# Row maxima of the scores by four row tiles of 32 rows, two units ahead, in an fp32 cross-attention kernel

## The chip, the cores and the metric

One core of a Trainium2 chip runs the kernel. The time is device microseconds of one execution, as the median of several runs; a profiled execution of the same program gives the trace. TensorE (PE) multiplies, with a record for each weight load (PEld) and each matmul; VectorE (DVE), ScalarE (ACT) and GpSimd (POOL) do the elementwise work, and SyncE (SP) issues the DMAs. Each engine works its own list of instructions in order, and semaphores are all that ties one list to another.

## The reference

Cross-attention with two branches of keys, added, then an output projection with bias and residual:

```python
text, ip = ctx[:, :77, :], ctx[:, 77:, :]          # x (2, 2048, 640), ctx (2, 154, 1024), all f32
q = split_heads(x @ Wq.T, 20)                       # 20 heads of 32
k, v = split_heads(text @ Wk.T, 20), split_heads(text @ Wv.T, 20)
k_ip, v_ip = split_heads(ip @ Wk_ip.T, 20), split_heads(ip @ Wv_ip.T, 20)
attend = lambda q, k, v: softmax(q @ k.T / sqrt(32)) @ v
out = merge_heads(attend(q, k, v)) + merge_heads(attend(q, k_ip, v_ip))
return out @ Wo.T + bo + x
```

## The kernel before

Channels lie on the partitions. A tile is 256 rows of x of one batch, and there are 16. A group is 128 channels, which are four heads of 32, and there are five. A unit is one group of one tile, so there are 80 units, `u`, written out ten at a time (two tiles) in a loop; `u.g` is its group. The softmax subtracts the row maximum of each head, branch and row. The maxima are taken from approximate scores (`q_hi`, the rounded q, against the keys), and enter the exact scores as two more rows of the contraction.

The sequence of each engine is written out by hand in its `emit(u)`, one call a unit, and a step for another unit stands at `u.plus(n)`. In emission u of the kernel before TensorE does, in order: the first two maxima products of u+1 (L735), the exact scores of heads 0 and 1 (L752), 8 of 15 steps of the q product of u+2 (L711), the third maxima product, scores of head 2, the fourth maxima product, more of q, scores of head 3, more of q, the transpose of the maxima of u+1 (L741), the rest of q, the 15 steps of an output chunk of unit u-10 (L711 again, into x_ps), the row sums of u (L769), its product with v (L780), and last the spreading of the inverse sums for unit u-5 (L789).

For a maxima product the kernel keeps `k_diag`, the keys of four heads on the diagonal of a 128 x 308 block with zeros elsewhere. One matmul of 128 x 308 gives the four heads of one branch for 128 rows; the two branches and the two halves of the tile make four matmuls a unit, which take turns in two PSUM banks, `a_ps`. VectorE reduces each (L571).

Once a tile, at `u.g == 0`, the row sums of the tile before are turned into inverses: ScalarE's `keep_sums` copies them (L422, behind the first two exponentials L405 and `keep_pv` L410), VectorE's `invert_sums` takes the reciprocal (L585) and splits it (L588, L590), which gives `inv_done`. The spread for group 0 of that tile waits for `inv_done`:

```python
def spread_inverse(u):
    if u.g == 0:
        wait(pe, inv_done, u.tile(INV_STEPS, INV_STEPS))
    wait(pe, scaled_done, u.number())
    wait(pe, y_done, u.number(1, 1 + SPREAD_LAG - OUT_LAG))
    spread_matmuls(u, x_ps)
```

VectorE's `normalise` (L598) then multiplies the spread inverses with the product with v. Every value for a product is kept as a rounded high part and a low part (fp32r), so that each product of q and of the output is 15 steps. Before the loop stand the key and value products of the context; in the first five units ScalarE and VectorE also split Wo (L464, L554).

Of the kernel before, what the change touches and what calls it, by code (L numbers as in the profile page):

```python
# [50 lines left out]
BLK = GROUP * KEYS  # L51
# [4 lines left out]
MAXES = SUB * BRANCHES  # L56
A_ITEMS = MAXES + 1
# [43 lines left out]
def build(nc, x_d, ctx_d, wq_d, wk_d, wv_d, wo_d, bo_d, out_d):  # L101
    with ExitStack() as stack:
# [20 lines left out]
        k_diag = sbuf("k_diag", [P, BRANCHES, GROUPS, BATCHES, GROUP, KEYS], F32R)  # L123
# [50 lines left out]
        zeroed = sem("zeroed")  # L174
# [20 lines left out]
        a_ready, a_drained = sem("a_ready"), sem("a_drained")  # L195
# [18 lines left out]
        K_ITEMS = BRANCHES * GROUPS  # L214

# [30 lines left out]
        def _(sp):  # L246
# [23 lines left out]
            def maxima(u):  # L270


                wait(sp, a_drained, u.number(A_ITEMS, A_ITEMS))
                sp.dma_start(q_stack[SHIFT_ROW:STACK, u.slot].bitcast(F32),
                             max_rows[:, u.slot, :].bitcast(F32)).then_inc(max_in[u.slot], DMA)
# [43 lines left out]
        def _(pool):  # L319
# [10 lines left out]
            nc.gpsimd.memset(k_diag[:, 1].bitcast(F32), 0.0).then_inc(zeroed, 1)  # L330
# [43 lines left out]
            add_branches(LAST.plus(-1))  # L374
# [9 lines left out]
        def _(act):  # L384
            def q_high(u):

                wait(act, q_acc, u.number(1, 1))
                wait(act, a_ready, u.number(A_ITEMS, -A_ITEMS))
# [77 lines left out]
            def keys_high(item):  # L466
# [5 lines left out]
                for j in range(GROUP):  # L472
                    rows = slice(j * D, (j + 1) * D)
                    done = nc.scalar.activation(
                        k_diag[rows, br, g, :, j, :],
                        k_banks[br][g % 2][rows, group_cols(g)].rearrange("p (b n) -> p b n", b=BATCHES),
                        ACT.Copy, scale=SCALE)
                done.then_inc(k_hi_done, 1)

            def keys_top(item):  # L480
# [3 lines left out]
                for j in range(GROUP):  # L484
                    nc.scalar.activation(k_stack[0:D, br, g * GROUP + j],  # L485
                                         k_diag[j * D:(j + 1) * D, br, g, :, j, :].bitcast(F32),
# [22 lines left out]
            act.wait_ge(zeroed, 2)  # L509
# [33 lines left out]
        def _(dve):  # L543
            nc.vector.memset(k_diag[:, 0].bitcast(F32), 0.0).then_inc(zeroed, 1)
# [21 lines left out]
            def max_piece(u, k):  # L566

                sub, br = divmod(k, BRANCHES)
                wait(dve, a_ready, u.number(A_ITEMS, k + 1))
                bank = a_ps[(u.c * A_ITEMS + k) % 2]  # L570
                nc.vector.tensor_reduce(row_max[:, u.slot, br, :, sub],  # L571
# [431 lines left out]
```

## Time and profile before

| | |
|---|---|
| time, median of 3 | 685.42 us (683.55 to 728.46) |
| the profiled execution's own time | 683.04 us |
| its span in the trace | 681.2 us |
| its mean granted TensorE clock | 0.989 of full |
| PE busy | 657.5 us, 97% of the span |
| DVE busy | 435.7 us, 64% |
| ACT busy | 493.3 us, 72% |
| POOL busy | 225.0 us, 33% |

The time is a little more than the span, which runs from the first to the last record. The row to look at is PE: matmul records overlap each other, so 97% says that TensorE hardly ever waits, and not that it is at its peak. The clock of the trace has two levels, 1.2 and 2.4 GHz, shown as 0.50 and 1.00.

### The profile page before, as it was taken

The page shows a single profiled execution, that of the slowest core. Times are in us where ns is not written, and L with a number is a line of the kernel's source. Part 1 is how long each engine was busy: PE and PEld are TensorE (multiplying, and loading weights), DVE is VectorE, ACT ScalarE, POOL GpSimd, SP SyncE. Part 2 cuts the span into 40 slices and gives each one's busy share as a digit, 9 for nine tenths or more (in the row PEclk, how much of TensorE's full clock was granted, in tenths as well). Part 3 has the DMA queues.
Part 4 walks back from the last instruction along what each step waited for, and adds up shares of the span by engine and source line. Part 5 has one row for each costly group of instructions (what it writes and reads, how often), then busy time and mean ns, then how long its engine had stood idle before and what let it go on. Part 6 is the DMA issues. An engine that isn't in the chain of part 4 may idle for free.

```text
span 681.2 us, 18904 instructions
## 1 busy us (share of the span) xinstructions
PE 657.5 (97%) x6514; PEld 564.5 (83%) x6514; DVE 435.7 (64%) x956; ACT 493.3 (72%) x1078; POOL 225.0 (33%) x261
## 2 busy tenths in 40 slices
PE   9959798999999999999999999999999999999997
PEld 9959576788888888888888888888888888888877
DVE  6786677675757566675756576665657566756633
ACT  3983787877868777877777787778777777876730
POOL 4020102243432434343434324343434243342333
PEclk9989898999999999999999999999999999999999
DMA  8950111223131221313131312213131323212212
GB/s 318 410 234 9 25 56 34 80 57 96 49 103 51 82 63 55 93 48 97 51 93 49 99 55 86 55 55 93 48 101 51 90 55 93 56 50 64 56 42 69
DMA packets 34691, 57.46 MB, mean 84 GB/s; under 512 B 4832, under 2 KB 27232, under 8 KB 34400
## 3 DMA queue, kind: packets, MB, share of 16 engines
q1 hardware_dynamic: 34656, 56.99, 27.3%
q8 instruction: 22, 0.36, 0.2%
q14 instruction: 13, 0.11, 0.0%
HBM read 35.34 MB, written 10.49 MB: 67 GB/s over the span
## 4 chain that ended last, share of the span: by engine, by line
PE 85%; DVE 6%; ACT 6%; issue 2%; POOL 0%; DVEq 0%; ACTq 0%
PE q_ps L711 19%; PE x_ps L711 19%; PE sum_ps L769 11%; PE b_ps L752 10%; PE pv_ps L780 10%; PE a_ps L735 7%; PE x_ps L789 5%; PE a_ps L741 1%; ACT probs L405 1%; DVE k_stack L631 1%; DVE k_stack L641 1%; ACT k_stack L485 1%; ACT q_stack L397 1%; DVE wo_lo L554 1%; DVE k_stack L545 1%
## 5 line engine op out<-in xcount | busy, mean ns | idle before, releaser
L405 ACT ACTIVATE probs<-b_ps 77x512 f32<-77x512 f32 x320 | 181.1, 591 | 121.0 <-PE b_ps L752 119.3
L562 DVE TENSOR_TENSOR q_stack<-q_ps,q_hi 32x256 fp32r<-32x256 f32 x320 | 134.3, 420 | 36.0 <-ACT q_hi L390 32.3
L571 DVE TENSOR_REDUCE row_max<-a_ps 128x4 f32<-128x308 f32 x320 | 137.6, 471 | 24.0 <-PE a_ps L735 21.3
L397 ACT ACTIVATE q_stack<-q_hi 32x256 fp32r<-32x256 f32 x320 | 133.0, 416 | 10.0
L598 DVE TENSOR_TENSOR scaled<-x_ps,pv_sb 128x512 f32<-128x512 f32 x75 | 51.9, 692 | 105.4 <-PE x_ps L789 105.0
L752 PE MATMUL b_ps<-q_stack,k_stack 98*77 98x256 f32 x640 | 115.1, 281 | 0.5 <-ACT probs L405 0.5
L347 POOL TENSOR_TENSOR scaled<-scaled 128x256 f32<-128x256 f32 x80 | 59.2, 740 | 139.1 <-DVE scaled L598 139.0
L352 POOL TENSOR_TENSOR attn_lo<-scaled,attn_hi 128x256 fp32r<-128x256 f32 x80 | 59.1, 739 | 113.2 <-ACT attn_hi L434 113.2
L358 POOL TENSOR_TENSOR res<-y,res 128x256 f32<-128x256 f32 x70 | 51.1, 731 | 136.8 <-ACT y L428 136.8
L735 PE MATMUL a_ps<-k_diag,q_hi 128*128 128x308 f32 x320 | 87.3, 313 | 7.0 <-DVE row_max L571 6.8
L752 PEld LDWEIGHTS b_ps<-q_stack,k_stack 98*77 98x77 f32 x640 | 85.7, 146 | 1.5 <-ACT probs L405 1.0
L711 PE MATMUL q_ps<-x_lo,wq_hi 128*128 128x256 f32 x400 | 86.7, 283 | 0.0
L780 PE MATMUL pv_ps<-probs,v 128*32 128x256 f32 x1280 | 84.3, 381 | 0.0
L769 PE MATMUL sum_ps<-probs,sum_one 128*32 128x256 f32 x1152 | 79.7, 390 | 1.2 <-ACT probs L405 1.2
L711 PE MATMUL q_ps<-x_hi,wq_hi 128*128 128x256 f32 x400 | 74.4, 283 | 6.6 <-POOL x_lo L341 6.3
L711 PE MATMUL q_ps<-x_hi,wq_lo 128*128 128x256 f32 x400 | 80.2, 298 | 0.0
L341 POOL TENSOR_TENSOR x_lo<-x_raw,x_hi 128x1280 fp32r<-128x1280 f32 x16 | 49.1, 3066 | 60.0 <-ACT x_hi L416 60.0
L711 PE MATMUL x_ps<-attn_hi,wo_hi 128*128 128x256 f32 x365 | 66.7, 280 | 0.8 <-DVE scaled L598 0.8
L711 PEld LDWEIGHTS q_ps<-x_lo,wq_hi 128*128 128x128 f32 x400 | 67.1, 192 | 0.0
L711 PE MATMUL x_ps<-attn_lo,wo_hi 128*128 128x256 f32 x365 | 66.6, 280 | 0.2 <-POOL attn_lo L352 0.2
L711 PE MATMUL x_ps<-attn_hi,wo_lo 128*128 128x256 f32 x365 | 66.5, 280 | 0.0
L780 PEld LDWEIGHTS pv_ps<-probs,v 128*32 128x32 f32 x1280 | 42.0, 111 | 28.4 <-issue 1.4
(111 smaller groups left out, 962.3 us busy)
## 6 DMA issues: line engine op xcount, KB each, us to landing
x_raw<-x_in SPq DMA_DIRECT2D x16, 640.0 KB, 4.2
q_stack<-q_stack SPq DMA_DIRECT2D x80, 128.0 KB, 2.3
res<-x_in SPq DMA_DIRECT2D x75, 128.0 KB, 2.0
y_out<-res SPq DMA_DIRECT2D x75, 128.0 KB, 1.7
stage<-wk_in SPq DMA_DIRECT2D x6, 640.0 KB, 7.9
stage<-wv_in SPq DMA_DIRECT2D x6, 640.0 KB, 10.7
wq_raw<-wq_in SPq DMA_DIRECT2D x1, 1600.0 KB, 10.2
wo_raw<-wo_in SPq DMA_DIRECT2D x1, 1600.0 KB, 14.6
```

Source lines behind the costliest of these rows:

```text
L347: nc.gpsimd.tensor_tensor(scaled[:, s, 0:N], scaled[:, s, 0:N], scaled[:, s, N:2 * N], ALU.add).then_inc(attn_done, 1)
L352: nc.gpsimd.tensor_tensor(attn_lo[:, u.batch, u.g, :], scaled[:, u.slot, 0:N], attn_hi[:, u.batch, u.g, :].bitcast(F32), ALU.subtract).the ...
L397: done = nc.scalar.activation(q_stack[0:D, u.slot, j, :], q_hi[j * D:(j + 1) * D, u.slot, :].bitcast(F32), ACT.Copy)
L405: nc.scalar.activation(probs[0:KEYS, j, :], b_ps[j % 2][0:KEYS, :], ACT.Exp).then_inc(b_drained, 1)
L562: done = nc.vector.tensor_tensor(q_stack[D:2 * D, u.slot, j, :], q_ps[rows, 0:N], q_hi[rows, u.slot, :].bitcast(F32), ALU.subtract)
L571: nc.vector.tensor_reduce(row_max[:, u.slot, br, :, sub], bank[:, 0:BLK].rearrange("p (j n) -> p j n", j=GROUP), AXIS.X, ALU.max).then_inc ...
L598: nc.vector.tensor_tensor(scaled[:, u.slot, :], bank[:], pv_sb[:, u.g, :], ALU.mult).then_inc(scaled_done, 1)
L711: return nc.tensor.matmul(out, (lo if kind == 1 else hi)(k), (moving_lo if kind == 2 else moving_hi)(k), start=(n == 0), stop=(n == STEPS_ ...
L735: nc.tensor.matmul(a_ps[(u.c * A_ITEMS + k) % 2][:, 0:BLK], q_hi[:, u.slot, sub * P:(sub + 1) * P], k_diag[:, br, u.g, u.batch].rearrange( ...
L752: done = nc.tensor.matmul(b_ps[j % 2][0:KEYS, br * N:(br + 1) * N], k_stack[0:STACK, br, u.g * GROUP + j, u.batch, :], q_stack[0:STACK, u. ...
L769: nc.tensor.matmul(sum_ps[j * D:(j + 1) * D, 0:N], sum_first[:] if first else sum_one[:, D - 1 - c:2 * D - 1 - c], probs[:, j, br * N:(br ...
L780: done = nc.tensor.matmul(pv_ps[j * D:(j + 1) * D, br * N:(br + 1) * N], v[:, br, u.batch, h * D:(h + 1) * D], probs[:, j, br * N:(br + 1) ...
```

## The change

Zero blocks go: `k_heads` holds the keys of a group as they come, 128 partitions with the four heads at 32 partitions each, both branches side by side. A maxima product is now one head, 32 rows deep, 128 rows of q wide, with 154 columns moving (77 keys of two branches). Eight such matmuls make a unit; four in turn lie in different row groups of the array and write to four PSUM banks (`b_ps` and `a_ps`). They come in one block, for unit u+2 and not u+1, between the output chunk and the row sums. VectorE's four reductions follow the low part of q. The spread goes from the end of the emission to between the q product and the output chunk, into the second `a_ps` bank and not `x_ps`; normalise follows in the same emission and not in the next, at group 0 behind `invert_sums`. Before the loop, two memsets of `k_diag` and three of four ScalarE copies of each key item go, and the maxima of unit 1 are made there.

```diff
-MAXES = SUB * BRANCHES
-A_ITEMS = MAXES + 1
+MAX_ITEMS = GROUP + 1
-        k_diag = sbuf("k_diag", [P, BRANCHES, GROUPS, BATCHES, GROUP, KEYS], F32R)
+        k_heads = sbuf("k_heads", [P, GROUPS, BATCHES, BRANCHES, KEYS], F32R)
+        max_banks = [*b_ps, *a_ps]
...
 gpsimd emit(u)
-                ahead, norm, chunk = u.tile_plus(1), u.plus(-1 - SPREAD_LAG), u.plus(-OUT_LAG)
+                ahead, norm, chunk = u.tile_plus(1), u.plus(-SPREAD_LAG), u.plus(-OUT_LAG)
+                if norm.plus(-1).exists():
+                    attn_low(norm.plus(-1))
                 if norm.exists():
                     add_branches(norm)
-                    attn_low(norm)
...
 scalar keys_high(item)
-                for j in range(GROUP):
-                    rows = slice(j * D, (j + 1) * D)
-                    done = nc.scalar.activation(
-                        k_diag[rows, br, g, :, j, :],
-                        k_banks[br][g % 2][rows, group_cols(g)].rearrange("p (b n) -> p b n", b=BATCHES),
-                        ACT.Copy, scale=SCALE)
-                done.then_inc(k_hi_done, 1)
+                nc.scalar.activation(k_heads[:, g, :, br, :],
+                                     k_banks[br][g % 2][:, group_cols(g)].rearrange("p (b n) -> p b n", b=BATCHES),
+                                     ACT.Copy, scale=SCALE).then_inc(k_hi_done, 1)
...
 vector
+            def max_piece(u, j, bank):
+                if not (u.fixed and u.number() == 0):
+                    wait(dve, max_ready, u.number(1, 1))
+                nc.vector.tensor_reduce(row_max[:, u.slot, :, j, :].rearrange("p r s -> p s r"),
+                                        bank[:, 0:SUB * BLK].rearrange("p (s r n) -> p s r n", s=SUB, r=BRANCHES),
+                                        AXIS.X, ALU.max).then_inc(max_read, 1)
...
             def emit(u):
-                norm, nxt = u.plus(-1 - SPREAD_LAG), u.plus(1)
-                if norm.exists():
-                    normalise(norm)
-                if nxt.exists():
-                    for k in range(MAXES):
-                        max_piece(nxt, k)
-                    max_turned(nxt)
+                norm, nxt = u.plus(-SPREAD_LAG), u.plus(1)
+                if nxt.exists():
+                    max_turned(nxt)
+                if norm.exists() and u.g != 0:
+                    normalise(norm)
                 if u.g == 0 and u.tile_plus(-1).exists():
                     invert_sums(u.tile_plus(-1))
+                if norm.exists() and u.g == 0:
+                    normalise(norm)
                 if u.plus(2).exists():
                     q_low(u.plus(2))
+                    for j in range(GROUP):
+                        max_piece(u.plus(2), j, max_banks[j])
...
 tensor
+            def max_matmuls(u, heads, banks):
+                for sub in range(SUB):
+                    for j, bank in zip(heads, banks):
+                        rows = slice(j * D, (j + 1) * D)
+                        done = nc.tensor.matmul(bank[:, sub * BLK:(sub + 1) * BLK],
+                                                q_hi[rows, u.slot, sub * P:(sub + 1) * P],
+                                                k_heads[rows, u.g, u.batch].rearrange("p r n -> p (r n)"),
+                                                start=True, stop=True, skip_group_check=True)
+                return done
+
+            def max_scores(u):
+                wait(pe, q_hi_done, u.number(1, 1))
+                wait(pe, max_read, u.number(MAX_ITEMS))
+                wait(pe, scaled_done, u.number(1, -1 - SPREAD_LAG))
+                wait(pe, b_drained, u.number(GROUP, -GROUP))
+                max_matmuls(u, range(GROUP), max_banks).then_inc(max_ready, 1)
...
 scores(u, j)
+                if j < 2 and u.plus(1).exists():
+                    wait(pe, max_read, u.number(MAX_ITEMS, MAX_ITEMS + j + 1))
...
 spread_inverse(u)
                 wait(pe, scaled_done, u.number())
-                wait(pe, y_done, u.number(1, 1 + SPREAD_LAG - OUT_LAG))
-                spread_matmuls(u, x_ps)
+                if u.plus(SPREAD_LAG + 1).exists():
+                    wait(pe, max_read, u.number(MAX_ITEMS, (SPREAD_LAG + 1) * MAX_ITEMS + GROUP))
+                spread_matmuls(u, a_ps[1])
...
 emit(u)
-                find_max(0)
-                find_max(1)
                 scores(u, 0)
+                project_q(u.plus(2), 0, 3)
                 scores(u, 1)
-                project_q(u.plus(2), 0, 8)
-                find_max(2)
+                project_q(u.plus(2), 3, 7)
+                if nxt.exists():
+                    turn_maxima(nxt)
                 scores(u, 2)
-                find_max(3)
-                project_q(u.plus(2), 8, 10)
+                project_q(u.plus(2), 7, 11)
                 scores(u, 3)
-                project_q(u.plus(2), 10, 13)
-                find_max(MAXES)
-                project_q(u.plus(2), 13)
+                project_q(u.plus(2), 11)
+                if norm.exists():
+                    spread_inverse(norm)
                 if chunk.exists():
                     project_out(chunk)
+                if u.plus(2).exists():
+                    max_scores(u.plus(2))
                 row_sums(u)
                 weigh_values(u)
-                if norm.exists():
-                    spread_inverse(norm)
...
 before the loop
+            pe.wait_ge(max_read, MAX_ITEMS)
+            wait(pe, q_hi_done, 2)
+            max_matmuls(first.plus(1), range(GROUP), max_banks).then_inc(max_ready, 2)
```

In the changed kernel BLK is 154 (`BRANCHES * KEYS`); it was 308.

## Rows read from the trace of the kernel before

**Rows 1.** Part 1 of the page: engine, busy us, share, instructions.
```profile
PE   657.5 (97%) x6514; PEld 564.5 (83%) x6514; DVE 435.7 (64%) x956; ACT 493.3 (72%) x1078; POOL 225.0 (33%) x261
```

**Rows 2.** Busy time by stage: window, us, then engines' busy us, PEclk.
```profile
302.00:377.00 75.00, 75.00 (x774) 64.21 (x773) 47.74 (x107) 57.29 (x126) 27.80 (x32) 1.00 0.25 71
```

**Rows 3.** Waits of TensorE over the span: total us, times, longest.
```profile
PE a_ps L735 <- DVE row_max L571: 6.8, 5, 3.9
```

**Rows 4.** Timeline of TensorE over one unit: start us, us, engine, line, records.
```profile
404.40 0.51 PE L789 MATMUL x_ps<-inv_parts,spread 128*128 128x256 f32 x2
...
409.88 0.28 PE L711 MATMUL x_ps<-attn_lo,wo_hi 128*128 128x256 f32 x1
410.10 1.07 PE L769 MATMUL sum_ps<-probs,sum_one 128*32 128x256 f32 x16
410.98 1.05 PE L780 MATMUL pv_ps<-probs,v 128*32 128x256 f32 x16
411.96 0.51 PE L789 MATMUL x_ps<-inv_parts,spread 128*128 128x256 f32 x2
412.31 0.44 PE L735 MATMUL a_ps<-k_diag,q_hi 128*128 128x308 f32 x2
412.59 0.64 PE L752 MATMUL b_ps<-q_stack,k_stack 98*77 98x256 f32 x4
413.06 0.64 PE L711 MATMUL q_ps<-x_hi,wq_hi 128*128 128x256 f32 x4
```

**Rows 5.** Weight loads by form: records, busy us, mean ns of one.
```profile
L711 PEld LDWEIGHTS q_ps<-x_hi,wq_hi 128*128 128x128 f32 x400 | 59.2, 190 | 7.3 <-issue 6.5 <-DVE q_stack L562 0.8
...
L741 PEld LDWEIGHTS a_ps<-ident,row_max 128*16 128x16 f32 x80 | 7.0, 88 | 0.6 <-DVE row_max L571 0.6
```

**Rows 6.** Timeline of weight loads, windows 395.07 to 395.09 and 395.11 to 395.13.
```profile
395.08 0.11 PEld L769 LDWEIGHTS sum_ps<-probs,sum_one 128*32 128x32 f32 x2
395.08 0.16 PEld L769 LDWEIGHTS sum_ps<-probs,sum_one 128*32 128x32 f32 x8
```

**Rows 7.** Timeline of TensorE before the loop, products with 154 columns moving.
```profile
57.69 1.47 PE L913 MATMUL b_ps<-ctx,stage 128*128 128x154 f32 x10
58.99 0.27 PE L741 MATMUL a_ps<-ident,row_max 128*16 128x128 f32 x1
```

**Rows 8.** Timeline of a unit of group 0, from its first scores on.
```profile
397.58 0.63 PE L752 MATMUL b_ps<-q_stack,k_stack 98*77 98x256 f32 x4
398.01 1.08 ACT L405 ACTIVATE probs<-b_ps 77x512 f32<-77x512 f32 x2 [0.62 <-PE b_ps L752]
...
399.46 0.39 ACT L422 ACTIVATE inv<-sum_ps 128x256 f32<-128x256 f32 x1
...
400.33 0.27 PE L741 MATMUL a_ps<-ident,row_max 128*16 128x128 f32 x1
...
400.94 1.73 DVE L585 RECIPROCAL inv<-inv 128x256 f32<-128x256 f32 x1
...
403.03 0.49 DVE L590 SCALAR_TENSOR_TENSOR inv_parts<-inv_hi,low_rows,inv 128x256 fp32r<-128x256 f32 x1
```

**Rows 9.** Timeline of TensorE in the first units: waits in brackets.
```profile
78.13 0.41 PE L735 MATMUL a_ps<-k_diag,q_hi 128*128 128x308 f32 x1 [3.86 <-DVE row_max L571]
...
105.43 0.41 PE L735 MATMUL a_ps<-k_diag,q_hi 128*128 128x308 f32 x1 [1.66 <-DVE row_max L571]
```

**Rows 10.** Busy time and clock by microsecond, columns as in Rows 2.
```profile
106.00:107.00 1.00, 1.00 (x9) 0.97 (x9) 0.74 (x2) 0.86 (x2) 0.00 (x0) 0.86 0.07 16
107.00:108.00 1.00, 1.00 (x9) 0.74 (x10) 0.52 (x2) 0.42 (x2) 0.00 (x0) 0.50 0.00 0
...
110.00:111.00 1.00, 1.00 (x17) 0.47 (x10) 0.95 (x3) 0.08 (x1) 0.00 (x0) 0.94 0.00 0
```

**Rows 11.** Timeline before and at the start of the loop.
```profile
47.04 1.19 PE L711 MATMUL q_ps<-x_hi,wq_hi 128*128 128x256 f32 x4 [6.30 <-POOL x_lo L341]
...
74.59 2.98 DVE L554 TENSOR_TENSOR wo_lo<-wo_raw,wo_hi 128x640 fp32r<-128x640 f32 x1 [1.99 <-ACT wo_hi L464]
```

More of the change, by code:

```diff
@@ L50 @@
 UNITS = TILES * GROUPS
-BLK = GROUP * KEYS
+BLK = BRANCHES * KEYS
 SHIFT_ROW = 3 * D
@@ L270, in maxima @@
             def maxima(u):
-                wait(sp, a_drained, u.number(A_ITEMS, A_ITEMS))
+                wait(sp, max_read, u.number(MAX_ITEMS, MAX_ITEMS))
                 sp.dma_start(q_stack[SHIFT_ROW:STACK, u.slot].bitcast(F32),
@@ L387, in q_high @@
                 wait(act, q_acc, u.number(1, 1))
-                wait(act, a_ready, u.number(A_ITEMS, -A_ITEMS))
+                wait(act, max_ready, u.number(1, -1))
                 wait(act, q_low_done, u.number(1, -1))
@@ L591, in invert_sums, with normalise @@
                                                in1=inv[:], op0=ALU.mult, op1=ALU.add).then_inc(inv_done, 1)
-            def normalise(u, bank=x_ps):
+            def normalise(u, bank=a_ps[1]):
                 wait(dve, inv_spread, u.number(1, 1))
@@ L671, in _ @@
             nc.vector.memset(probs[64:P], 0.0).then_inc(probs_zeroed, 1)
-            for k in range(MAXES):
-                max_piece(Unit(0, 0), k)
+            for j in range(GROUP):
+                dve.wait_ge(first_max_ready, j // 2 + 1)
+                max_piece(Unit(0, 0), j, a_ps[j % 2])
             dve.wait_ge(v_zeroed, 1)
@@ L682, in _ @@
                 place_v(item)
+            for j in range(GROUP):
+                max_piece(Unit(0, 1), j, max_banks[j])
             dve.wait_ge(bo_loaded, DMA)
@@ L686, in _ @@
             stages(emit)
-            normalise(LAST.plus(-1))
             invert_sums(LAST)
@@ L727, in project_q @@
                     done.then_inc(q_acc, 1)
-            def max_scores(u, k):
-                sub, br = divmod(k, BRANCHES)
-                if k == 0:
-                    wait(pe, q_hi_done, u.number(1, 1))
-                wait(pe, a_drained, u.number(A_ITEMS, k - 1))
-                nc.tensor.matmul(a_ps[(u.c * A_ITEMS + k) % 2][:, 0:BLK], q_hi[:, u.slot, sub * P:(sub + 1) * P],
-                                 k_diag[:, br, u.g, u.batch].rearrange("p j n -> p (j n)"),
-                                 start=True, stop=True).then_inc(a_ready, 1)
+            def max_matmuls(u, heads, banks):
[13 more added lines that the diff above has]
+                max_matmuls(u, range(GROUP), max_banks).then_inc(max_ready, 1)
             def turn_maxima(u):
-                wait(pe, a_drained, u.number(A_ITEMS, MAXES))
-                nc.tensor.transpose(a_ps[(u.c * A_ITEMS + MAXES) % 2][0:BRANCHES * SUB * GROUP, 0:P],
-                                    row_max[:, u.slot].rearrange("p r j s -> p (r j s)"), ident[:]).then_inc(a_ready, 1)
+                wait(pe, max_read, u.number(MAX_ITEMS, GROUP))
+                nc.tensor.transpose(a_ps[0][0:BRANCHES * SUB * GROUP, 0:P],
+                                    row_max[:, u.slot].rearrange("p r j s -> p (r j s)"), ident[:]
+                                    ).then_inc(max_turned_over, 1)
             def scores(u, j):
@@ L948, in _ @@
             project_ip_values(1, 4)
-            max_scores(first, 0)
-            max_scores(first, 1)
+            wait(pe, q_hi_done, 1)
+            max_matmuls(first, (0, 1), a_ps).then_inc(first_max_ready, 1)
             project_ip_values(4, 5)
-            max_scores(first, 2)
-            max_scores(first, 3)
+            wait(pe, max_read, 2)
+            max_matmuls(first, (2, 3), a_ps).then_inc(first_max_ready, 1)
             project_ip_values(5, 6)
```

33 lines of the change are left out of this document (10 added, 23 removed).

## The prediction

> **What bounds the kernel now.** I read the page's busy times first: TensorE is busy 657.5 of 681.2 us and no other engine over 72% [rows 1]. The window of a middle stretch says it harder: 75.00 of 75.00 us busy at clock 1.00 [rows 2]. The view of waits then shows what TensorE waited for: its largest item is 6.8 us in five waits, the maxima products for VectorE's reductions [rows 3], and the two that the timeline places at 78.13 and 105.43 make 5.5 of them, in the first units [rows 9]. So in the loop the time is the sum of TensorE's own steps, and every wait that the change puts into TensorE's list is paid in full.
>
> The timeline gives the price of each step as distance from start to start, since records overlap. A unit lasts 411.96 - 404.40 = 7.56 us; four score matmuls take 413.06 - 412.59 = 0.47, or 0.117 each (256 columns, fp32r); two maxima matmuls of 308 columns take 0.28, or 0.14 each; the row sums 0.88 for 16 records, the product with v 0.98, the two spread matmuls 0.35; the last output step to the first sum 0.22 where 0.12 would be its own share [all rows 4]. The 0.10 beyond it, the 0.98 against 0.88, and the 0.35 against 2 x 0.117 are what a change of the array's tiling costs: about 0.10 before the first load, and for a 128-column load another 0.12 that no matmul hides.
>
> **The change part by part.**
>
> *Maxima on TensorE.* Gone: 4 x 0.14 = 0.56 us a unit [rows 4]. New: eight matmuls of 154 columns in two rounds of four. No row tile stands in the trace, so I bound it. The nearest rows are the column tiles of the row sums: eight weight loads start within 0.05 us (0.16 less the 0.11 of one), some 7 ns apart [rows 6], and 16 records of 256 columns take 0.88 us, a quarter of what they would one after another [rows 4]. If row tiles do the same, a round costs what one matmul does. A load costs by its width: (190 - 88) ns for 112 more columns [rows 5], so about 0.12 us for 128. One pass over 154 columns is 154/256 of 0.117, 0.07 us. The block: first load 0.12, second load 0.12 (the first round lies under it), second round 0.07, sum 0.31. It has another tiling than the output chunk and than the row sums, so there are two changes where there was one: +0.10. The spread, now between two products of the full array, loses its 0.12 of bare load; instead the scores follow the product with v and bare a 77-column load, +0.07. In all -0.56 + 0.31 + 0.10 - 0.12 + 0.07 = -0.20 a unit. The steps of the old unit add up to 39 x 0.117 (30 product, 8 score and the transpose) + 0.56 + 0.35 + 0.10 + 0.88 + 0.98 = 7.43, so 0.13 of this 7.56 was small waits, mostly of the two-bank ping-pong of maxima and reductions; the unit before took less, so I count 0.05 of them, and they go. That makes -0.25 x 80 = -20 us.
>
> The other end has two places. The same trace runs a product of 154 columns in plain f32 as two records of (58.99 - 57.69)/10 = 0.13 [rows 7], 0.26 a product; all its fp32r products move 256 columns or more. If fp32r at 154 columns is run like f32, the block is 0.12 + 2 x 0.26 = 0.64 and not 0.31, +26 us over 80 units. If the eight 128-column loads go one after another, it is 8 x 0.12 + 0.07 = 1.03, +58 us. Below 0.31 nothing goes much: the gain would be 0.56 + 0.05 at most with a free block, 0.3 more than I take. I take 0.31 since the column tiles are the nearest rows.
>
> The Trainium skill's page "TensorE: Matmul & The Clock Gate", section "What overlaps and what doesn't", speaks against it: a weight load overlaps matmuls in flight only where its row group differs. The second round's loads would then wait for the first round, 0.38 for the block and 5 us more in all. The trace shows the contrary where it can: loads of the same column tile start before its matmul has run [rows 6], so I leave the sum as it is.
>
> *Two units ahead, and four banks.* Reductions are four of about the same size as before. Max_scores waits for the rounded q, for the reads of u+1's maxima and their transpose, for normalise of u-5 (it read that bank), and for the last exponential. By TensorE's list there are a spread and an output chunk, 0.23 + 1.76 = 2 us, between the q product and it, against one ScalarE copy or one normalise of under 0.7; no wait. The next unit's first scores wait for the first reduction; row sums and product with v, 1.9 us, cover it and q_low's four pieces. In the first ten units, without chunks, the cover is thinner. Cost nothing, 1 us at most a unit of those.
>
> *The spread moved forward.* This is the step that decides. In group-0 units the spread needs `inv_done` of the tile before, whose chain starts in the same emission. From the unit's first scores at 397.58: first exponential at +0.43, keep_sums at +1.88, the transpose of the maxima at +2.75, the reciprocal at +3.36 behind the turned maxima, the last step ends at 403.03 + 0.49, +5.94 [rows 8]. The spread was at 404.40, +6.82, so 0.88 us in hand. In the new order: scores of head 1 start at 0.23 + 0.35 = 0.58, so the second exponential at 1.01, keep_pv 1.49, keep_sums 1.97. Reciprocal to end of the split is 2.58 in the trace; VectorE is free after the turned maxima (transpose at 1.28, read till about 1.96), so the reciprocal starts 0.4 behind the copy, at 2.4, and inv_done comes at 4.96, TensorE goes on at 5.05. But it arrives at 8 scores, 15 q steps and a transpose, 24 x 0.117 = 2.8. Wait: 2.25 us, behind which the whole output chunk, the maxima, sums and product with v are queued, and ScalarE and VectorE behind those. TensorE has no slack to give it back. Tiles with such a spread inside the loop: 15 (units 5, 10, ... 75). +34 us. In the other four groups the spread waits for nothing late.
>
> *The clock.* Behind the wait of 1.66 us at 105.43 the granted clock goes to 0.50 (1.2 GHz) from about 106.7 to 110.1 [rows 9, 10]: 3.4 us at half speed, 1.7 us lost. The new waits are longer, 2.25, and come once in five units. I count the fall behind 12 of 15, since one row is thin evidence for each: 12 x 1.7 = +20 us; bounds 0 and 15, +26.
>
> *Start.* ScalarE's key copies fall from four to one an item and two memsets go, which pulls forward the low part of x that TensorE waited 6.30 us for at 47.04 [rows 11]. But TensorE's wait of 3.86 at 78.13 is for VectorE, busy with the low part of Wo until 77.57, and that waited for ScalarE and its input [rows 9, 11]; what is gained before runs into it. New order leaves it somewhat further in its list by then, and the wait of 1.66 falls in with the first new one. Against it, the first scores of unit 0 now wait for the first reduction of unit 1. I take -4, bounds 0 and -9.
>
> Sum against the profiled execution's 683.0: -20 - 4 + 34 + 20 = +30, 713 us. The median of the runs shown is 685.4, 0.3% above that execution, so it is the same measure.
>
> **Rivals.**
>
> *The clock stays up.* All as above, but waits of 2.25 us don't bring it down: 683 - 20 - 4 + 34 = 693, range 688 to 699, +1% and so not slower by what can be told. For it: a busy block before and behind each wait. Against: the row at 106.7. It decides at how many of the 15 the clock falls; below 4 of them the result is under 699.
>
> *f32 pace at 154 columns.* +26 on the forecast: 739 (719 with the clock up). For it: no fp32r row under 256 columns. Against: the type, not the width, parts the rows there are.
>
> *Loads one after another.* +58: 771 (751 with the clock up). For it: a load's time goes by its width. Against: the column tiles' loads.
>
> *The other side.* TensorE reaches the spread late instead of waiting there. Scores of heads 2 and 3 wait for the first two exponentials, and head 0 for the DMA of the maxima; were TensorE held at one of these in every group-0 unit by 2 us while ScalarE, already past the exponentials, goes on with keep_sums, the chain would be as good as done on arrival. It decides from a rest of the wait under 0.5 us; that leaves 7 of the 34 us, no fall of the clock, and 683 - 20 - 4 + 7 = 666. Against it: the DMA is asked for 1 us earlier in the unit than now, and by the new order the exponentials end (1.0 and 1.6) before the scores that need them (1.4 and 2.1).
>
> **How the numbers follow.** Forecast 713 (701 to 722): 0.45. Clock up: 0.16. f32 pace: 0.15. Loads in turn: 0.13. Wait absent or small: 0.05. Else, spread about: 0.06. Low 688 takes in the clock rival, high 752 the f32 pace and the mild end of the loads rival; left out are the 666 case and most of the loads rival, about 0.18. Some two per cent is what a measurement of this kernel can tell from no change: faster (under 671.7) 0.05, within (to 699.1) 0.21, slower 0.74.
>
> **What would show it.** The spread record (L789's like) of every fifth unit with an idle of about 2.25 us before it, released by the split of the inverse on VectorE, 15 times; ScalarE's keep_sums some 2 us and the reciprocal some 2.4 us behind the unit's first scores. Granted clock 0.50 for 3.4 us behind most of them, mean near 0.96 in the loop. Ordinary units of 7.2 to 7.3 us. The maxima block, from its first load to the first load of the row sums, 0.3 + 0.1; eight records of 154 columns each, starting in fours some 7 ns apart. Records in twos would be f32 pace, starts 0.1 apart would be loads in turn. I am wrong if the chain's end comes before TensorE arrives, or if max_scores or the first scores wait for reductions in ordinary units.

## The result, and the profile after

The changed kernel takes 730.84 us, median of four, against 685.07: ratio 1.0676, interval 1.064 to 1.0712. One of the four executions of the kernel before was a slow one of 728.46 us, and the ratio leaves it out (the other three have a median of 684.72). The changed kernel's profiled execution took 729.86, its span is 728.1 us at a mean granted clock of 0.957, against 681.2 at 0.989.

The view of waits, beside [rows 3], tells most of it (engine, line, who was waited for: total us, times, longest):

```profile
PE a_ps L799 <- DVE inv_parts L584: 27.0, 15, 2.2
PE b_ps L762 <- issue: 14.9, 5, 3.0
PE b_ps L732 <- DVE scaled L592: 4.9, 5, 1.0
PE q_ps L709 <- POOL x_lo L342: 3.7, 1, 3.7
```

The first row is the forecast wait of the spread, 15 times. The second stands in no part of the prediction: TensorE stops before the first scores of a loop pass, five times for about 3 us, and the profile shows no other engine that it waits for ("issue"). From here on it is called the stop at the back edge, which is the jump from the end of a pass to the start of the next. The third is the maxima product of units 5 to 9, which waits for normalise.

All rows of that view add up to 60.1 us; for the kernel before they make 19.4. The clock's loss is (1 - 0.957) x 728.1 = 31.3 us against (1 - 0.989) x 681.2 = 7.5. So of 728.1 - 681.2 = 46.9 us, 40.7 are waits, 23.8 are clock, and the rest, -17.6, is what is left for faster work.

An ordinary unit, beside [rows 4], timeline of TensorE (start us, us):

```profile
402.52 0.40 PE L799 MATMUL a_ps<-inv_parts,spread 128*128 128x256 f32 x2
402.75 0.64 PE L709 MATMUL x_ps<-attn_hi,wo_hi 128*128 128x256 f32 x4
...
404.42 0.28 PE L709 MATMUL x_ps<-attn_lo,wo_hi 128*128 128x256 f32 x1
404.63 0.34 PE L732 MATMUL b_ps<-k_heads,q_hi 32*128 32x154 f32 x2
404.63 0.34 PE L732 MATMUL a_ps<-k_heads,q_hi 32*128 32x154 f32 x2
404.80 0.27 PE L732 MATMUL b_ps<-k_heads,q_hi 32*128 32x154 f32 x2
404.81 0.27 PE L732 MATMUL a_ps<-k_heads,q_hi 32*128 32x154 f32 x2
405.01 1.07 PE L779 MATMUL sum_ps<-probs,sum_one 128*32 128x256 f32 x16
...
409.78 0.40 PE L799 MATMUL a_ps<-inv_parts,spread 128*128 128x256 f32 x2
```

Read the starts: from spread to spread 7.26 us. The unit of [rows 4] took 7.56, but it is the longest of its tile: five units of the kernel before, from the scores at 397.58 to those at 434.94, take 37.36 us, 7.47 each. The two spreads take 0.23 (before 0.35); four maxima matmuls start together at 404.63, the second four at 404.80, and the sums at 405.01. From 404.63 to 405.01, less the 0.10 of the next change of tiling, is 0.28 us for eight matmuls. They are one record each, where plain f32 had two [rows 7], so fp32r with 154 columns is one pass here.

Their loads, beside [rows 6]:

```profile
404.63 0.18 PEld L732 LDWEIGHTS b_ps<-k_heads,q_hi 32*128 32x128 f32 x2
404.63 0.18 PEld L732 LDWEIGHTS a_ps<-k_heads,q_hi 32*128 32x128 f32 x2
404.73 0.19 PEld L732 LDWEIGHTS b_ps<-k_heads,q_hi 32*128 32x128 f32 x2
404.74 0.19 PEld L732 LDWEIGHTS a_ps<-k_heads,q_hi 32*128 32x128 f32 x2
```

Four loads of 128 columns start within 0.01 us, four more 0.10 later, while the first matmuls still run by their records: row tiles load side by side as the column tiles do.

A unit of group 0, beside [rows 8]:

```profile
421.41 0.46 PE L762 MATMUL b_ps<-q_stack,k_stack 98*77 98x256 f32 x2
...
423.47 0.38 ACT L423 ACTIVATE inv<-sum_ps 128x256 f32<-128x256 f32 x1
...
423.88 1.75 DVE L579 RECIPROCAL inv<-inv 128x256 f32<-128x256 f32 x1 [0.43 <-ACT inv L423]
...
424.19 0.28 PE L709 MATMUL q_ps<-x_lo,wq_hi 128*128 128x256 f32 x1
...
426.00 0.48 DVE L584 SCALAR_TENSOR_TENSOR inv_parts<-inv_hi,low_rows,inv 128x256 fp32r<-128x256 f32 x1
426.53 0.70 PE L799 MATMUL a_ps<-inv_parts,spread 128*128 128x256 f32 x2 [2.06 <-DVE inv_parts L584]
```

Against the first scores: keep_sums at +2.06 (forecast 1.97), reciprocal +2.47 (2.4), spread +5.12 (5.05). The wait reads 2.06 since the profile counts it from the end of the last matmul's record; from that matmul's start, 424.19, to the spread's are 2.34 us, less the 0.12 that a step takes 2.22, and the forecast was 2.25.

In the first unit of a pass it looks otherwise:

```profile
299.79 0.46 PE L762 MATMUL b_ps<-q_stack,k_stack 98*77 98x256 f32 x2 [2.97 <-issue]
300.08 0.61 PE L709 MATMUL q_ps<-x_hi,wq_hi 128*128 128x256 f32 x3
...
304.09 0.28 PE L709 MATMUL q_ps<-x_lo,wq_hi 128*128 128x256 f32 x1
305.46 0.50 PE L799 MATMUL a_ps<-inv_parts,spread 128*128 128x256 f32 x2 [1.10 <-DVE inv_parts L584]
```

The inverse is no earlier here (spread at +5.67), but TensorE has come to it later: its last step ends at +4.57 where it ended at +3.06 above, for behind the stop it runs at half clock.

And the clock behind such waits, beside [rows 10] (window, us, engines' busy us, PEclk):

```profile
263.00:265.00 2.00, 2.00 (x10) 1.79 (x9) 1.86 (x5) 0.00 (x0) 0.73 (x1) 0.50 0.29 66
306.00:308.00 2.00, 2.00 (x23) 1.82 (x21) 1.85 (x4) 0.94 (x3) 0.73 (x1) 1.00 0.12 25
427.00:429.00 2.00, 2.00 (x12) 2.00 (x11) 1.58 (x4) 0.17 (x1) 0.73 (x1) 0.50 0.29 66
634.00:636.00 2.00, 2.00 (x27) 1.70 (x29) 1.93 (x5) 0.48 (x1) 0.74 (x1) 1.00 0.33 74
```

In the two microseconds behind the 15 waits it stood at 0.50 nine times and at 1.00 six times; behind all five stops at the back edge it stood at 0.50. One of the nine lies in a stretch that a stop had begun (215.0 to 225.3). Of the ten waits of 2.06 to 2.24 us seven had the half clock behind them.

### The profile page after: what moved, and what is told of

Read it like the earlier page. It is cut to its first block, busy times and chain, and to the rows that moved or that the text cites. A ratio compares the mean times of both kernels' runs of the same rounds, so it can differ in the third digit from the quotient of the medians.

```text
span 728.1 us, 19277 instructions
## 1 busy us (share of the span) xinstructions
PE 662.8 (91%) x6834; PEld 559.5 (77%) x6834; DVE 433.8 (60%) x955; ACT 481.3 (66%) x1048; POOL 221.6 (30%) x260
## 4 chain that ended last, share of the span: by engine, by line
PE 76%; DVE 13%; issue 5%; ACT 3%; DMA 1%; SPq 0%; DVEq 0%; ACTq 0%; POOL 0%
PE x_ps L709 17%; PE q_ps L709 17%; PE b_ps L762 11%; PE sum_ps L779 10%; PE pv_ps L790 9%; PE b_ps L732 4%; DVE inv L579 4%; PE a_ps L799 3%; DVE q_stack L557 2%; DVE k_stack L637 2%; DVE row_max L565 1%; DVE k_stack L627 1%; PE a_ps L918 1%; PE a_ps L748 1%; DVE inv_parts L584 1%
## 5 line engine op out<-in xcount | busy, mean ns | idle before, releaser
L406 ACT ACTIVATE probs<-b_ps 77x512 f32<-77x512 f32 x320 | 189.1, 594 | 149.3 <-PE b_ps L762 148.2
L762 PE MATMUL b_ps<-q_stack,k_stack 98*77 98x256 f32 x640 | 143.4, 307 | 18.8 <-issue 14.9
L592 DVE TENSOR_TENSOR scaled<-a_ps,pv_sb 128x512 f32<-128x512 f32 x75 | 51.9, 692 | 96.2 <-PE a_ps L799 96.2
L573 DVE CAST max_rows<-a_ps 16x128 fp32r<-16x128 f32 x80 | 22.3, 278 | 134.6 <-PE a_ps L748 134.6
L709 PE MATMUL q_ps<-x_hi,wq_hi 128*128 128x256 f32 x400 | 89.0, 289 | 3.7 <-POOL x_lo L342 3.7
L709 PE MATMUL q_ps<-x_hi,wq_lo 128*128 128x256 f32 x400 | 88.8, 289 | 0.0
L565 DVE TENSOR_REDUCE row_max<-b_ps 128x4 f32<-128x308 f32 x158 | 68.4, 475 | 10.2 <-PE a_ps L732 8.0
L709 PE MATMUL x_ps<-attn_lo,wo_hi 128*128 128x256 f32 x365 | 71.0, 294 | 0.3 <-POOL attn_lo L353 0.3
L709 PEld LDWEIGHTS q_ps<-x_hi,wq_hi 128*128 128x128 f32 x400 | 66.8, 196 | 4.0 <-issue 3.9
L565 DVE TENSOR_REDUCE row_max<-a_ps 128x4 f32<-128x308 f32 x162 | 69.3, 471 | 0.6 <-PE a_ps L732 0.5
```

Of the source, the lines that this page charges most:

```text
L406: nc.scalar.activation(probs[0:KEYS, j, :], b_ps[j % 2][0:KEYS, :], ACT.Exp).then_inc(b_drained, 1)
L565: nc.vector.tensor_reduce(row_max[:, u.slot, :, j, :].rearrange("p r s -> p s r"), bank[:, 0:SUB * BLK].rearrange("p (s r n) -> p s r n", ...
L592: nc.vector.tensor_tensor(scaled[:, u.slot, :], bank[:], pv_sb[:, u.g, :], ALU.mult).then_inc(scaled_done, 1)
L709: return nc.tensor.matmul(out, (lo if kind == 1 else hi)(k), (moving_lo if kind == 2 else moving_hi)(k), start=(n == 0), stop=(n == STEPS_ ...
L762: done = nc.tensor.matmul(b_ps[j % 2][0:KEYS, br * N:(br + 1) * N], k_stack[0:STACK, br, u.g * GROUP + j, u.batch, :], q_stack[0:STACK, u. ...
```

## The experiments

Each was measured beside the kernel before on the same chip; that one's medians there were 683.6 to 684.5 us. "Records" are those of TensorE in one pass of the loop, with its weight loads and those instructions for waiting and counting that the trace records. "Packets" are the transfers of instructions over the whole execution, about 16 KB each (22 make 0.36 MB in the kernel before).

**e1: the spread back at the end.** PE emission (normalise, GpSimd and the guarding waits follow as in the kernel before):

```diff
-                if norm.exists():
-                    spread_inverse(norm)
                 if chunk.exists():
                     project_out(chunk)
...
                 weigh_values(u)
+                if norm.exists():
+                    spread_inverse(norm)
```

> The changed kernel with one part undone: the spread of the inverse sums stands again at the end of the emission, into the bank of the output chunk, and normalise follows in the next emission, as before the change; the row tiles, four banks and two units ahead stay. My account of the changed kernel's 730.8 us: 15 waits for the inverse, 27.0 us in its trace; five waits of 0.99 us of the maxima for normalise in units 5 to 9; the clock at half for 61 us against 14 before, which loses 24 us more than before; and five stops of 3 us at the loop's back edge put down to issue. Theory A (the waits and the clock falls behind them are the spread's place): the 15 and the five waits go, most clock falls with them, the stops at the back edge stay, the spread bares its weight load again (+7): 730.8 - 27 - 5 - 19 + 7 = about 687 us. Rival B (the clock falls come from the row tiles, not from the waits): the half-clock stretches stay, about 706 us. Rival C (another wait takes their place, since the inverse was only the first of several late steps): 715 us or more.

Measured 689.23 us, ratio 1.0083 (1.0061 to 1.0105). No wait for the inverse is left; this is:

```profile
PE b_ps L760 <- issue: 15.2, 6, 3.1
PE b_ps L731 <- ACT q_hi L391: 6.5, 9, 1.0
```

The clock is 0.986 over 687.3 us, a loss of 9.6 and not 31.3. Theory A, 2 us above its 687: 42 us of the result belong to the spread's place, and about half of them are clock. The waits of units 5 to 9 stayed in another form (for the rounded q: 6.5 us against 1.9 in the changed kernel), where A had them go. The stops stayed, and four of the five long ones have a half-clock stretch behind them.

**e2: fewer waits in TensorE's loop.** In `max_scores`, `scores` and `spread_inverse`, waits implied by others stand only outside the loop (`u.fixed` is true there), as in

```diff
-                wait(pe, b_drained, u.number(GROUP, -GROUP))
+                if u.fixed:
+                    wait(pe, b_drained, u.number(GROUP, -GROUP))
```

> The changed kernel, with seven waits a unit left out of TensorE's list inside the loop, each met already by an earlier wait of the same list or chain, so nothing else moves. TensorE's loop body has 1620 matmul and load records as before this edit, but by the program some 100 instructions fewer in all, about as many as the kernel before has. The changed kernel stops five times for 3 us at the loop's back edge, and its trace shows instruction transfers all through the loop, 68 packets against 22 of the kernel before, which shows none between 213 and 595 us. Theory A (the body has outgrown what stays resident, and is fetched again in each pass): stops and transfers go, 5 x 3.0 us and the half-clock stretch behind each (5 x 1.7 at most): 707 to 716 us. Rival B (the stops come from the new order, whatever the length): within 2 us of 730.8, transfers unchanged. Rival C: the edit isn't large enough, transfers and stops stay, 726 to 731 us.

726.20 us, ratio 1.0613 (1.0572 to 1.0655). Five stops, 14.8 us, 67 packets: rival C. The edit made 1738 records a pass out of 1780.

**e3: the wait filled with work.**

```diff
+FILL = 19
...
                 if u.g == 0:
+                    wait(pe, y_done, u.number(1, SPREAD_LAG - OUT_LAG))
+                    for _ in range(FILL):
+                        nc.tensor.matmul(x_ps[:, 0:N], wq_hi[:, 0, 0:P], x_hi[:, u.batch, 0, :], start=True, stop=True)
                     wait(pe, inv_done, u.tile(INV_STEPS, INV_STEPS))
```

> The changed kernel with 19 matmuls of no use (256 columns, into the output chunk's bank, before the chunk starts) ahead of each spread of group 0, so that TensorE works where it waited for the inverse; the wait for the inverse follows them. Nothing of the result changes. 19 x 0.117 = 2.2 us, as long as the wait. Theory A (idle time of 2 us brings the clock down, and that costs 1.7 us each): the waits shrink to under 0.3 us, as much time is used as before the edit, but the half-clock stretches behind them go, 11 or so of 15: 730.8 - 15 to -19 = 712 to 716 us. Rival B (the clock goes down whatever TensorE does there): 730 to 733 us with as many half-clock stretches. Rival C: the matmuls delay the inverse chain itself: over 735 us.

733.73 us, ratio 1.0714 (1.0693 to 1.0736), where A said 712 to 716 and B 730 to 733. One of the four executions took 3223.3 us; it has no trace, and what it did is open (the other three: 733.03 to 734.00). The time misses A by 18 us and lies nearest to B, and the trace says otherwise. First its clock behind two filled waits, then its waits:

```profile
432.00:434.00 2.00, 2.00 (x19) 1.97 (x18) 1.27 (x4) 0.73 (x2) 0.50 (x1) 1.00 0.09 23
264.00:266.00 2.00, 2.00 (x40) 1.08 (x40) 1.96 (x6) 0.43 (x1) 0.73 (x1) 1.00 0.04 8
```

```profile
PE b_ps L763 <- issue: 15.4, 5, 3.3
PE q_ps L710 <- issue: 9.2, 5, 2.0
```

No wait for the inverse, and no fall of the clock behind any of the 15; the loss by clock is (1 - 0.973) x 732.2 = 19.8 us and not 31.3. But 78 records more in a pass come with a second stop behind the first, 9.2 us. Fill +33.6 (15 x 2.24), waits -27.0, clock -11.5, second stop +9.2: +4.3, and the spans differ by 4.1 (the fit is closer than its terms, for a wait that reads 2.06 costs 2.2 from start to start). So it is the idle time that brings the clock down. A had priced the clock only: a fill longer than the waits that it replaced, and the second stop, took back what the clock gave.

**e4: the kernel before, with a longer loop.**

```diff
+PAD = 9
...
                 row_sums(u)
+                if not u.fixed:
+                    for _ in range(PAD):
+                        wait(pe, b_drained, u.number(GROUP, 1))
                 weigh_values(u)
```

> The kernel before, with nine more waits a unit in TensorE's list inside the loop, all on a semaphore value that is met already, 90 instructions a pass of ten units, so that the loop body is as long as the changed kernel's. Theory A (length alone makes the loop fetch its instructions anew and stop at the back edge): transfers of instructions all through the loop, five stops of about 3 us, perhaps a half-clock stretch behind each: 685 + 15 to + 24 = 700 to 709 us. Rival B (length is harmless, the stops belong to the new order): 685 to 687 us, no transfers between 213 and 595 us. If the waits themselves take time in TensorE's list, 0.05 us each, up to 27 us more appear as longer units, and the trace tells them apart.

Median 705.37 us of 708.28, 708.80, 702.46 and 688.66, too far apart for a ratio. Only the first was traced: it has four stops, 14.8 us, 58 packets and 1739 records. That the one of 688.66 us ran without stops is likely by its clock (0.990 against 0.972) and not shown. The trace has both cases in itself, though: between 444 and 527 us no instructions are transferred, and the back edge in that stretch, at 452, is the one without a stop. So the stops need nothing of the change, and they come and go with the transfers. The 90 waits more a pass are only 50 records more: a record isn't an instruction, and all counts below are of records.

**e5: e1 with a shorter loop.** Edit as in e2, on e1, for nine waits.

> The kernel of e1 (spread at the end of the emission again), with nine waits a unit less in TensorE's loop, each implied by another wait that stays. e1 measured 689.2 us; of that, five or six stops of 3 us at the loop's back edge (15.2 us in its trace) and three half-clock stretches behind them. Its loop pass had 1769 TensorE records, the kernel before 1689 without a stop, e2 1738 and the lengthened kernel before (e4) 1739 with stops. This one should have about 1715. Theory A (a body of so many records stays resident): no instruction transfers inside the loop, 689 - 15 - 5 = 667 to 671 us, which would be 2% faster than before. Rival B (the limit lies below 1715): stops stay, 685 to 689 us. Rival C (a wait left out did hide something): slower than 690 us.

690.87 us, ratio 1.0107 (1.009 to 1.0124), 1722 records, five stops, 13.3 us. The time is 2 us over B's range and just in that of rival C; by the trace it is B, the stops stay. Of what C supposes the trace shows little: 4.9 us of waits of the first scores for VectorE's reductions, against 3.0 in e1. Leaving waits out gives nothing by itself either.

**e6: the heads in turn.**

```diff
-                for sub in range(SUB):
-                    for j, bank in zip(heads, banks):
+                for j, bank in zip(heads, banks):
+                    for sub in range(SUB):
```

> The kernel of e1, with the eight maxima matmuls of a unit in another order: the two halves of one head one behind the other, then the next head, so that matmuls next to each other lie in the same row group. Same instructions, same number. In e1 the four heads start within 0.02 us. Theory A (four row tiles run side by side only if they follow each other; TensorE starts in order): the second matmul of a head waits for its own load, 0.12 us, and holds the next head back; the block takes about 0.6 us and not 0.28, +0.3 x 80 = 24 us, 710 to 716 us. Rival B (the array sorts it out, loads of other row groups run ahead): 0.3 us, 688 to 691 us.

690.66 us, ratio 1.01 (1.0083 to 1.0117), within 1.5 us of e1: rival B. Its timeline:

```profile
406.06 0.28 PE L708 MATMUL x_ps<-attn_lo,wo_hi 128*128 128x256 f32 x1
406.27 0.34 PE L731 MATMUL b_ps<-k_heads,q_hi 32*128 32x154 f32 x2
406.29 0.34 PE L731 MATMUL a_ps<-k_heads,q_hi 32*128 32x154 f32 x2
406.45 0.28 PE L731 MATMUL b_ps<-k_heads,q_hi 32*128 32x154 f32 x2
406.46 0.28 PE L731 MATMUL a_ps<-k_heads,q_hi 32*128 32x154 f32 x2
406.67 0.64 PE L777 MATMUL sum_ps<-probs,sum_first 128*32 128x256 f32 x8
```

0.40 us from the first to the sums, where the order by halves takes 0.38. Neighbours in the list need not lie in different row groups.

**e7: only group 0 back.** As e1, but `if u.g == 0` at the end and `u.g != 0` in the middle, with the banks to match, and eleven waits left out.

> The changed kernel, with the spread at the end of the emission (into the output chunk's bank, normalise in the next emission) only in units of group 0, where the inverse comes late; in the other four groups it stays between the q product and the output chunk. Eleven or so waits a unit less in TensorE's loop, each implied by another, about 1708 records a pass. Theory A: no wait for the inverse, no stop at the back edge; against e5 four of five spreads keep their load covered, 0.1 us each, 60 of them, 6 us less: 661 to 665 us. Rival B (as for e5: the body is still too long): 680 to 684 us. Rival C (normalise of group 0 now meets that of group 1 in one emission and pushes VectorE or GpSimd late): over 690 us.

688.68 us, ratio 1.0067 (1.005 to 1.0085), 1711 records, five stops, 14.8 us. By the stops it is rival B, but 5 us over its 680 to 684: the rest of the edit saves 2 us against e5, where I had reckoned with 6.

**e8, e9, e10: only the place of the loop.** After eight kernels with the stop, of 1711 to 1858 records, against one of 1689 without, it was either the length or the place of the body in the list. Small matmuls go before the loop, 44 in e8 (on e2), 48 in e9 (on e7), 35 in e10 (on the kernel before):

```diff
             project_ip_values(0, 1)
+            for _ in range(44):
+                nc.tensor.matmul(q_ps[0:16, 0:16], ident[:, 0:16], ident[:, 0:16], start=True, stop=True)
             pe.wait_ge(wq_lo_done, 1)
```

> The kernel of e2 with nothing changed in the loop: 44 matmuls of no use (16 columns, f32, four records each) stand before the loop, where TensorE waits for the low part of x anyway, and shift its list by 176 records. Counted in blocks of 256 records (an instruction transfer is 16 KB, 64 bytes each), the loop of the kernel before began at 8.02 and ended at 14.61, seven blocks, 8 to 14, and was not fetched again. Those of the changed kernel (8.41 to 15.36), e1 (8.45 to 15.36), e2 (8.41 to 15.20), e5 (8.42 to 15.14) and e7 (8.40 to 15.09) touch eight blocks, and all stop at the back edge; e4 began at 7.98. This one goes from 9.10 to 15.89, seven blocks, with e2's body of 1738. Theory A (seven blocks stay, eight don't): no transfers inside the loop, no stops, 726.2 - 14.8 - about 7 of clock = 703 to 707 us. Rival B (it is the number of records in the body, limit between 1693 and 1711): stops stay, 724 to 729 us.

> The kernel of e7, its loop untouched, with 48 such matmuls before the loop: its start goes from 8.40 to 9.15 blocks and its end to 15.84, seven blocks instead of eight. Theory A (blocks touched): 688.7 - 14.8 for the stops - up to 8.5 for half-clock stretches (20.4 us of them against 3.4 where nothing stops) = 664 to 669 us, 2 to 3% faster than the kernel before. Rival B (length of the body): 687 to 690 us.

> The kernel before, its loop untouched, with 35 such matmuls before the loop, where TensorE waits 6.3 us anyway: start from 8.02 to 8.56 blocks, end from 14.61 to 15.16, eight blocks instead of seven. Theory A: transfers of instructions all through the loop, stops of 3 to 4 us at the back edge, half-clock stretches behind some: 684 + 15 to + 24 = 699 to 708 us. Rival B (length of the body): 683 to 686 us, no transfers between 213 and 595 us.

e8: 725.87 us, ratio 1.0613 (1.0583 to 1.0642). e9: 691.50 us, 1.0109 (1.0092 to 1.0126). Both with stops (14.5 and 14.4 us); e8 is in rival B's range, e9 1.5 us over it. e10: 711.31 us, 1.0399 (1.0382 to 1.0417), 3 us over theory A's 699 to 708, and this one rules rival B out, for its loop is that of the kernel before, instruction for instruction. Its waits, and its transfers of instructions on the page (queue: packets, MB, share):

```profile
PE a_ps L735 <- issue: 16.9, 9, 3.0
PE a_ps L735 <- DVE row_max L571: 6.9, 5, 3.8
```

```profile
q8 instruction: 67, 1.10, 0.6%
```

The same line of the kernel before has 22 packets, none of them between 202 and 585 us. The added matmuls take 1.9 us inside a wait for x that was there before. By the spans it is 29.9 us longer than the kernel before: 16.9 are stops, 11.0 clock by the means. So the place decides. What was wrong in e8 and e9 may then be only the zero of my count, and e11 tests that.

**e11 and e12: the place worked out from the failures.**

> The kernel of e7 once more, loop untouched, now with 30 small matmuls before the loop (e9 had 48). e10 showed that a shift alone of the kernel before, with the same body, brings the stops; e8 and e9 showed that the block borders don't lie where whole numbers of my count lie. If seven blocks stay and eight don't, the runs bound the place of the border in the count: before (8.02 to 14.61) without stops puts it at a fraction between .62 and 1.02; e9 (9.15 to 15.84) with stops takes away all from .83 up, e4 (7.98 to 14.79) all from .79. So a border lies at a fraction of .62 to .79. This kernel goes from 8.87 to 15.55, which is seven blocks for every border in that stretch. Theory A (blocks touched): no transfers inside the loop, no stops, 688.7 - 14.8 - 5 to 8.5 = 664 to 669 us, 2 to 3% faster than before. Rival B (a shift matters in another way, or 1711 records are too many wherever they lie): 687 to 692 us.

669.43 us, ratio 0.9781 (0.9765 to 0.9798): 2.2% faster than the kernel before, and 19 us less than e7 with the same loop. Its packets and its largest waits:

```profile
q8 instruction: 23, 0.38, 0.3%
```

```profile
PE b_ps L772 <- DVE row_max L567: 5.9, 14, 1.9
PE b_ps L735 <- ACT q_hi L393: 4.2, 7, 1.0
```

No stop at the back edge; from 215 to 595 us the clock is 1.00. With e7 and e9 this is one loop at three places: 688.68, 691.50 and 669.43 us.

> The kernel of e2 (order of the changed kernel, waits for the inverse and all; seven redundant waits a unit left out), with 28 small matmuls before the loop: from 8.85 to 15.64 in my count, seven blocks for a border at a fraction of .63 to .79. e11 fell from 688.7 to 669.4 us by the same kind of shift, e8 (44 of the matmuls, wrong place) not at all. Theory A: no transfers in the loop, no stops at the back edge, 726.2 - 19 = 705 to 709 us; what then stays above the kernel before, 21 to 25 us, is the price of the moved spread less the gain of the row tiles. The half-clock stretches behind the waits for the inverse stay. Rival B (with the inverse waits in, the stop at the back edge only hides another wait of the same length): 715 us or more.

714.78 us, ratio 1.0424 (1.0357 to 1.0491), executions from 709.03 to 718.82. Between the two theories by its median: the profiled execution has two stops, 8.3 us, in the first passes, then none (41 packets, none between 371 and 616 us). Its loop is e2's, 1738 records, and by the count it ends at 15.64, 0.09 blocks beyond e11, so it left little room below eight blocks; e4, just as tight, varied in the same way. That tight fits settle late is what these two suggest and is not shown further. Once the stops are gone the wait for the inverse is 2.08 us in the first unit of a pass too, and a pass takes 78.6 us (spreads at 385.33, 463.95, 542.56) where the kernel before takes 74.7. So the moved spread costs about 4 us a pass, clock included, after the gain of the row tiles; for 80 units that is an estimate of 31.

## Why the prediction was right, and what it left out

- *The spread's place* decided, as said. Forecast 15 waits of 2.25, 34 us; there were 15, ten of 2.06 to 2.24 and five, in the first units of the passes, of 0.7 to 1.7: 27.0 us. These five are shorter since TensorE reached the spread late, at half clock behind the stop, and not since the inverse was early. e1 shows that without the 15, and with the clock back, 42 us go.
- *The clock.* Forecast: 12 falls of the 15, +20 us. Found: behind the 15 waits eight half-clock stretches of their own, 15.4 us lost (the ninth wait fell into a stop's stretch), and behind the stops another 11.9. That the whole came to +23.8 and so near to 20 is luck: one part was counted too high and the other not at all. e3 shows that idle time does it: with work in the wait it never fell there.
- *The row tiles.* Forecast 0.31 us for the block, found 0.28; a unit 0.25 us less, found 0.22 (7.47 to 7.25), which makes 17.6 us over 80 units, as much as the rest above. Both rivals of price, f32 pace and loads in turn, are dead: each of the eight matmuls has one record, and four loads start within 0.01 us. The rule I weighed against the trace, from the Trainium skill's page "TensorE: Matmul & The Clock Gate", section "What overlaps and what doesn't", says that a load overlaps running matmuls only where its row group differs; here the second four loads went to the same four row groups 0.10 us behind the first, under their matmuls.
- *The start.* Forecast -4, bounds 0 and -9. TensorE comes to unit 5's first scores at 97.45 us and not at 102.16, 4.7 less, and the old wait of 1.66 at 105.43 is gone with its 1.7 of clock: -8, a part of which is the row tiles' own.
- *"No wait" at the maxima product.* Right from unit 10 on, and for units 5 to 9 I had said 1 us at most: 0.99 each, 4.9 us. It should have been in the sum.
- *What was left out.* The stops were in no part of the sum: TensorE's loop body, once moved in its list, was transferred again in each pass, 14.9 us of stops and 11.9 of clock behind them, 27 in all. The weak step is "the time is the sum of TensorE's own steps": I priced 40 more matmuls and loads a pass by their time on the array and never asked where the loop lay. e10 prices this alone: 28 us on a kernel whose loop is unchanged.

Added up, what was found is 27.0 + 15.4 - 17.6 - 8 + 4.9 + 14.9 + 11.9 = 48.5 us, against 46.9 between the spans; the row tiles' part of the start is in it twice. The forecast's centre of 713 is near what the change costs without the stops: e12, with the changed kernel's order, seven waits a unit fewer and most stops gone, took 709 to 719 us.

The measured 730.8 is beyond the 701 to 722 of the forecast itself. It lies in the whole range only because that was wide for another reason, the unknown price of row tiles; that much was luck. The count in e11's expectation (a block of 256 records, seven stay, eight don't) was built on failures and then gave 669.43, half a microsecond above its 664 to 669. That the place of the loop decides is shown by e10 and by e7, e9 and e11; the number seven is inferred from counts of records, which leave instructions out, and no run tests it by itself. The Trainium skill's page "Advanced Engine Details and Errata", section "ISA Cache", gives TensorE 128 KB in lines of 16 KB, 256 instructions; that makes eight lines, an estimate from its figures, and by my count the loops that stayed touch seven. The same section says "Only 2 cache lines!", and the kernel before differs: its loop of 1689 records, 6.6 such lines, ran from 202 to 585 us without a transfer.

## What to carry to other kernels

Before a step is moved forward, find the last chain that feeds it and where in the same pass that chain starts: 0.88 us of slack at the old place was the warning, and here the bound engine paid the wait twice, 27.0 us as idle time and 15.4 as clock. Keep the late case (one group of five) where it was and move the rest: e7 did, and had no wait for the inverse. And where a change makes a long loop body longer or moves it in its list, compare the instruction transfers of the traces before and after: if they now run on inside the loop (68 packets here against 22), shift the loop by some 30 small matmuls, as e11 did, before you judge the change.

## What was not expected of the hardware

- Thirty-five small matmuls ahead of the loop made an unchanged loop 28 us slower (683.6 to 711.3), and thirty made another 19 us faster (688.7 to 669.4).
- In one execution of e4 and one of e12 some passes have instruction transfers and a stop at the back edge, and others have neither.
- Eight matmuls in four row tiles take the same 0.38 to 0.40 us, up to the row sums, whether their order alternates row groups or not.
- Stops of 3 us at the back edge had the half clock behind them each time in the changed kernel and four times of five in e1, while waits of 2.06 to 2.24 us did in seven of ten, and in seven of thirteen in e12.
- Four loads of 128 columns into four row groups start within 0.01 us, and four more 0.10 us later.
